# First self attention of a two-layer decoder: queries, keys and outputs by three fp32r products each, queries and keys by way of DRAM

## The reference

```python
xq = jnp.einsum('bsh,oh->bso', x, wq)
xk = jnp.einsum('bsh,oh->bso', x, wk)
xv = jnp.einsum('bsh,oh->bso', x, wv)
xq = xq.reshape(bsz, N_HEADS, seqlen, HEAD_DIM)
...
scores = jnp.einsum('bhid,bhjd->bhij', xq, xk) * SCALE
scores = jax.nn.softmax(scores, axis=-1)
out = jnp.einsum('bhij,bhjd->bhid', scores, xv)
out = out.reshape(bsz, seqlen, N_HEADS * HEAD_DIM)
return jnp.einsum('bso,ho->bsh', out, wo)
```

## Time and profile before

| | |
|---|---|
| median of 3 runs | 3024.14 us (3023.61 to 3031.14) |
| the profiled execution, whole | 3019.45 us |
| its span, first to last instruction | 3017.7 us |
| mean granted TensorE clock | 0.944 |
| TensorE busy | 2672.6 us, 89% |
| VectorE, ScalarE, GpSimd busy | 1675.6, 1177.9, 1563.1 us |
| DMA | 142460 packets, 238.12 MB |

### The profile page before, as it was taken

How to read it: one execution, slowest core, us unless ns; L and a number is a source line. 1 busy time by engine, 2 the same in 40 slices (tenths; PEclk the granted TensorE clock), 3 DMA queues, 4 the chain that set the end, 5 groups by cost and what they waited for, 6 DMA issues and landing times. The chain is left out here.

```text
span 3017.7 us, 40593 instructions
## 1 busy us (share of the span) xinstructions
PE 2672.6 (89%) x11441; PEld 1597.7 (53%) x11441; DVE 1675.6 (56%) x3323; ACT 1177.9 (39%) x1638; POOL 1563.1 (52%) x1298
## 2 busy tenths in 40 slices
PE   7999999999999999999999968982795588689696
PEld 5666666666666666666666533431574244333264
DVE  5665656655566556665665634662234555358753
ACT  3444444444444444444444324541222333345334
POOL 2666676667766677666766841224334212222353
PEclk9999999999999999999999979996897599899798
DMA  4333332333223332333323320003893100000143
GB/s 132 72 79 72 83 72 65 82 78 81 68 71 82 71 82 65 72 83 78 72 69 79 77 75 16 2 2 119 340 341 131 39 1 1 30 2 9 33 139 90
DMA packets 142460, 238.12 MB, mean 79 GB/s; under 512 B 27638, under 2 KB 72990, under 8 KB 137246
## 3 DMA queue, kind: packets, MB, share of 16 engines
q1 hardware_dynamic: 126510, 166.81, 22.2%
q0 software_dynamic: 11904, 64.06, 6.0%
q10 hardware_dynamic: 3952, 6.08, 0.6%
HBM read 89.52 MB, written 29.38 MB: 39 GB/s over the span
## 5 line engine op out<-in xcount | busy, mean ns | idle before, releaser
L636 POOL TENSOR_TENSOR a_total<-a_total,a_pr 128x1024 f32<-128x1024 f32 x384 | 912.6, 2377 | 70.3 <-ACT a_pr L620 49.9
L620 ACT ACTIVATE a_pr<-a_psS 128x1024 f32<-128x1024 f32 x512 | 525.1, 1026 | 650.2 <-PE a_psS L608 646.4
L567 DVE TENSOR_REDUCE a_nmax<-a_psX 128x1 f32<-128x512 f32 x1024 | 694.3, 687 | 149.7 <-PE a_psX L562 147.2
L648 PE MATMUL a_psO<-a_pr,a_vd 128*64 128x512 f32 x2048 | 481.8, 602 | 0.0
L562 PE MATMUL a_psX<-a_kA,a_qA 128*128 128x512 f32 x1024 | 412.3, 403 | 8.0 <-DMA a_kA<-a_klo 4.6
L636 POOL TENSOR_TENSOR a_total<-a_pr 128x1024 f32<-128x1024 f32 x64 | 152.9, 2388 | 507.1 <-ACT a_pr L620 507.1
L608 PE MATMUL a_psS<-a_qA,a_kA 128*128 128x512 f32 x1024 | 346.6, 420 | 1.6 <-DVE a_nT L583 1.4
L608 PE MATMUL a_psS<-a_qB,a_kB 128*128 128x512 f32 x1024 | 320.2, 394 | 0.7 <-DVE a_qB L591 0.7
L648 PEld LDWEIGHTS a_psO<-a_pr,a_vd 128*64 128x64 f32 x2048 | 129.9, 136 | 248.3 <-issue 212.0
L608 PEld LDWEIGHTS a_psS<-a_qA,a_kA 128*128 128x128 f32 x1024 | 183.7, 188 | 123.8 <-issue 90.1
L562 PEld LDWEIGHTS a_psX<-a_kA,a_qA 128*128 128x128 f32 x1024 | 191.9, 187 | 91.2 <-DVE a_nmax L567 16.5
(11 more groups left out here) (366 smaller groups left out, 4206.3 us busy)
## 6 DMA issues: line engine op xcount, KB each, us to landing
a_qA<-a_qhi SPq DMA_DIRECT2D x256, 128.0 KB, 2.3
a_kA<-a_khi SPq DMA_DIRECT2D x128, 128.0 KB, 2.3
a_kA<-a_klo SPq DMA_DIRECT2D x128, 128.0 KB, 2.3
a_kB<-a_khi SPq DMA_DIRECT2D x128, 128.0 KB, 2.3
a_qB<-a_qlo SPq DMA_DIRECT2D x128, 128.0 KB, 2.3
a_vd<-a_vg SPq DMA_DIRECT2D x128, 128.0 KB, 2.3
sorted_in<-g_zero SPq DMA_DIRECT2D x4, 1280.0 KB, 10.3
e_xg<-sorted_in SPq DMA_DIRECT2D x40, 128.0 KB, 7.5
```

The source lines that it names most:

```text
L567: w.eng.tensor_reduce(nmax[:, half, u:u + 1], psX[:, half, :], AX.X, ALU.max, negate=True)\
L620: w.eng.activation(pr[:, n, :], psS[:, half, :, :].rearrange("p a b -> p (a b)"), ACT.Exp, scale=SCALE)\
L636: w.eng.tensor_tensor(total[:, buf, :], first, pr[:, n, :], ALU.add).then_inc(sems["ad"], 1)
L648: last = w.eng.matmul(psO[q * HD:(q + 1) * HD, :], vd[:, b, kc, :], pr[:, n, q * 512:(q + 1) * 512], start=kc == 0, stop=kc == KC - 1)
```

## The change

Weights wq, wk and wo are split before the loop in a high part and a rest, as wv was. A piece of queries or keys is now six products (high with high, high with rest, rest with high, two halves of x), one of outputs 24. The parts of queries and keys go from a ring of four pieces (`ph`, `pl`) to DRAM, two transfers of 128 x 4 x 256 bytes per piece, and `build` reads six transfers of 256 KB from there; it waits for all stores issued before. The attention output is split by a new function, `split_out`, two units after it was computed. Output pieces move to place "1" of units 1 and 3, query and key pieces to other places, and the norm's parts move with them.

```diff
-        PLACES = [(3, "1"), (3, "3"), (3, "3b"), (3, "3c"), (3, "3d"), (0, "1"), (0, "3"), (0, "3b"),
-                  (1, "1"), (1, "3"), (1, "3b"), (1, "3c"), (1, "3d"), (2, "1"), (2, "2"), (2, "2b")]
+        PLACES = [(3, "3"), (3, "3b"), (3, "3c"), (3, "3d"), (0, "1"), (0, "2"), (0, "2b"), (0, "3"), (0, "3b"), (0, "3c"),
+                  (0, "3d"), (1, "3"), (1, "3b"), (1, "3c"), (1, "3d"), (2, "1")]
-            slots[0, "3d"] = slots[2, "3b"] = ("O",)
+            slots[1, "1"] = slots[3, "1"] = ("O",)
...
-                    for cc in range(2):
-                        last = w.eng.matmul(ps[:, 0:GT], wt[:, cc, c * P:(c + 1) * P], xT[:, cc, :],
-                                            start=cc == 0, stop=cc == 1)
+                    for n, (wp, xp) in enumerate(((hi, xh), (hi, xl), (lo, xh))):
+                        for cc in range(2):
+                            last = w.eng.matmul(ps[:, 0:GT], wp[:, cc, c * P:(c + 1) * P], xp[:, cc, :],
+                                                start=n == 0 and cc == 0, stop=n == 2 and cc == 1)
...
-                    for c in range(KC):
-                        last = w.eng.matmul(ps[:, 0:D], oT[:, buf, c, :], wo[:, c, :], start=c == 0, stop=c == KC - 1)
+                    for n, (op, wp) in enumerate(((oh, woh), (oh, wol), (ol, woh))):
+                        for c in range(KC):
+                            last = w.eng.matmul(ps[:, 0:D], op[:, buf, c, :], wp[:, c, :],
+                                                start=n == 0 and c == 0, stop=n == 2 and c == KC - 1)
...
                 if w.on("scalar"):
-                    if what == ("Q", 0) and not fresh:
-                        taken(w)
                     w.wait("mi", w.at("mi"))
-                    w.eng.activation(dst(hi), src, ACT.Copy).then_inc(sems["ch"], 1)
+                    w.wait(f"so{n}", w.at(f"so{n}"))
+                    w.eng.activation(ph[:, n, :], ps[:, 0:GT], ACT.Copy).then_inc(sems["ch"], 1)
...
+                if w.on("sync"):
+                    c, row = what[1], w.fixed(G * (GH * P))
+                    w.waits(("md", w.at("md", -1)))
+                    for t, src in ((qhi, ph), (qlo, pl)) if kind == "Q" else ((khi, ph), (klo, pl)):
+                        w.eng.dma_start(t[bass.ds(row, GH * P), c * HD:(c + 1) * HD].rearrange("(h p) t -> p h t", p=P),
+                                        src[:, n, :].bitcast(F32).rearrange("p (h t) -> p h t", t=HD)).then_inc(sems[f"so{n}"], 16)
...
-                w.waits(("md", w.at("md")), ("s", w.at("s")))
+                w.waits(("s", w.at("s")), *((f"so{n}", w.at(f"so{n}")) for n in range(PIECES)))
...
-                    for par in range(2):
-                        w.eng.dma_start(t[rows:rows + HD, b, par * 512:(par + 1) * 512].bitcast(F32),
-                                        src[par * HD:(par + 1) * HD, bass.ds(gbuf, 1), j, :].bitcast(F32)).then_inc(sems[f"{n}{b}"], 16)
+                    w.eng.dma_start(t[rows:rows + HD, b, :].bitcast(F32).rearrange("p (s n) -> p s n", n=512),
+                                    src[bass.ds(row, P), :].rearrange("(s p) n -> p s n", p=HD)).then_inc(sems[f"{n}{b}"], 16)
...
+        def split_out(w, j):
+
+            t, cols = j // 2, slice(j % 2 * HD, (j % 2 + 1) * HD)
+            if w.on("scalar"):
+                w.wait("ot", w.at("ot"))
+                w.wait("y", w.at("y"))
+                w.eng.activation(oh[:, t, :, cols], oT[:, :, :], ACT.Copy).then_inc(sems["oh"], 1)
+            w.inc("oh")
+            if w.on("vector"):
+                w.wait("oh", w.at("oh"))
+                w.eng.tensor_tensor(ol[:, t, :, cols], oT[:, :, :], oh[:, t, :, cols].bitcast(F32), ALU.subtract)\
+                    .then_inc(sems["ol"], 1)
+            w.inc("ol")
...
-                        if outs and kc == 2:
+                        if outs and kc == 6:
                             root(w, 1 if j == 1 else 0)
-                        if outs and kc == 5:
-                            norm_out(w, G - (j == 1), 1 if j == 1 else 0)
+                        if kc == 1 and (j == 2 or j == 0) and not first:
+                            norm_out(w, G - 1, 1 if j == 2 else 0)
...
-                        if outs and kc == 1:
+                        if outs and kc == 5:
                             moments(w, 1 if j == 1 else 0)
                         piece(f"k{kc}")
+                        if older and kc == 1:
+                            split_out(w, (j - 2) % GH)
```

More of the change, by code:

```diff
@@ L670, in turn_back, with divide @@
             w.inc("rec")
-        def divide(w, j):
+        def divide(w):
             if w.on("gpsimd"):
@@ L688, in group @@
                 old = not (first and j == 0)
+                older = not (first and j < 2)
                 def step(i):
@@ L704, in piece @@
                     ahead = 2 if task == ("T",) or j == 3 else 1
-                    if task is None or (not old if task[0] == "O" else ahead > left):
+                    if task is None or (first and j == 1 if task[0] == "O" else ahead > left):
                         return under
                     if task[0] == "O":
-                        misc(w, task, G - (j == 0), 1 if j == 0 else 0, bank=bank, back=under)
+                        misc(w, task, G - (j == 1), 1 if j == 1 else 0, bank=bank, back=under)
                     else:
```

102 lines of the change are left out of this document (50 added, 52 removed).

## The result

The changed kernel takes 3285.3 us (median, 3271.1 to 3288.7) against 3024.1 (3023.6 to 3031.1): a ratio of 1.084, interval 1.082 to 1.086. I had forecast 3104, 3045 to 3185. The direction was right and the mechanism in part, the size was not: 261 us came where I had 80. Neither of the two signs that I had named for a wrong forecast appeared: the search doesn't run at 0.70 through kc 2 and 3, and waits for DMA stand ahead of it in two of the four units from 500 to 620 us.

The account below looks back on a forecast made before the run. TensorE's work and waits were taken as the bound. Per group -4.0 + 1.5 + 0.95 + 6.1 = +4.6 us, 70 over the groups, with 10 before the loop +80: forecast 3104 us, range 3045 to 3185.

Parts of the forecast that it names:

- the two signs: Forecast wrong if the search runs at 0.70 through kc 2 and 3, or DMA waits precede it in every unit.
- What bounds the kernel: In the loop, what TensorE executes or waits for is the stage's time; it is busy 99.6 of 100 us.
- The products: fp32r products of 256 columns on TensorE take 0.120 us each, gaining 3.45 us per group.
- What moves away: VectorE's moments go behind reduction 11, gaining 0.25 us; unit 0's output piece no longer waits 0.3 us for its bank.
- What comes back at the unit's end: At the ends of units 0, 1 and 3 VectorE sets the next search's start: 1.5 us per group lost.
- The 0.95 us for unit 2's missing cover: Unit 2 loses its output piece, so the second score pass waits for the masked maxima: 0.95 us with x's subtraction.
- The split of the attention output: VectorE's `ol` after reduction 3 waits for ScalarE's copy and delays search matmul 6: 6.1 us per group, the largest term.
- The way over DRAM: Stores and loads of queries and keys fit beside the loop's work: cost 0 in the sum.
- the bound of 32 us: Upper bound for the DRAM way: 1 us in each of units 0 and 2, 32 us in all.
- Before the loop: Weight splits, 32 stores and the build put the first search at 45 us instead of 35.7: 10 us.
- The rival of the stores: Dear 256-byte stores or late builds cost 3 to 4 us per group and 25 at the beginning: 3185; chance 0.16.
- The split hides: Rival: `oh` is ready before reduction 3 ends, the split costs under 1 us per group: 3009 or 2995; chance 0.12.

Follow-up runs that it names:

- e1: The changed kernel with VectorE's subtraction `ol` on 128 x 64 columns in place of 128 x 512; 3238.6 us.
- e4: The changed kernel with GpSimd's add of kc 1 on 64 of 1024 columns; 3158.8 us.
- e11: The changed kernel with ScalarE's copy `oh` alone moved into the tail of the unit before; 3081.7 us.
- e2: The changed kernel with the copy `oh` moved into the tail of the unit before and subtraction `ol` moved from VectorE to GpSimd; 3065.5 us.
- e5: e2 with GpSimd's four operations for the root moved behind the last add, after the masked maxima are written; 3034.7 us.
- e8: e5 with the build at the end of unit 0 no longer waiting for the last four stored pieces of the next group; 3032.7 us.
- e9: e8 with the splits of the value and output weights moved behind all first projections; 3024.1 us, ratio 0.9988 to the kernel before.
- e14: e9 with the value pieces of units 0 and 1 at kc 7 and the splits of wq and wk in halves; 3028.2 us, ratio 0.9983.
- e12: e9 with four value pieces moved behind the last scores of units 0, 1 and 2, x's transposes last in the tail; 3031.1 us, ratio 1.0005.
- e10: e5 with query and key products in fp32 again, their DRAM way and places kept; 3045.7 us.
- e7: The kernel before the change with only the moments, root and normalised output moved; 3051.1 us.
- e6: The kernel before the change with only the way of queries and keys over DRAM added; 3031.9 us.

## Why the prediction missed

- **What bounds the kernel:** right. TensorE sets the end, and from the change over e1, e4, e11, e2, e5, e8 to e9 and e14 each version's stage is shorter as its waits ahead of the search are. e12 is the exception: its new waits stand elsewhere.
- **The products:** right, 0.12 us each. For the output 1.3 us per group (forecast 1.15). Of the 2.3 us for queries and keys 0.9 reached the loop's length (e10); with the 1.5 that come back at the units' ends, the sum had 0.8.
- **What moves away** is the first step that failed: "They go to behind reduction 11 [...]: 0.25 us gained." I followed the moments on VectorE and never the four operations of the root on GpSimd, from kc 2 to kc 6. There they delay the last add into the masked write. e5 puts it at 33.6 us of the stage; e7, with the moments and the normalised output moved too, at 20.0.
- **What comes back at the unit's end:** right for VectorE's part, as just said. The 0.95 us for unit 2's missing cover was a wait for the masked maxima; what stands there is a wait for loads, 1.2 us in e9's unit 2.
- **The split of the attention output** is the step that made the miss: "the subtraction, as `xl`, 0.68". `xl` runs while GpSimd is idle (it starts at 670.69 in unit 2's tail, and the last add ends at 667.07); `ol` was put just behind exponential 1, whose end starts GpSimd's add. The place and the chain over ScalarE held. The waits did not: 2.70, 2.87, 1.38 and 2.69 us in units 3, 0, 1 and 2 of one group, where I had 1.28, 1.87, 1.11 and 1.87, and unit 3 is off the most, because a copy that is earlier, but not early enough for the subtraction to start ahead of the add, only makes it stand longer. Without the add the term costs 94.5 us (e4 to e2; the sum had 95, partly by luck). With it, it costs 213 (the change to e2): 76 us more of idle TensorE, and 43 more of busy time at the lower clock, a term that the sum didn't have at all.
- **The way over DRAM:** hidden in the kernel before (e6), as said, with 9.5 us of waits; 36.7 in the change and 39.1 in e5, over the bound of 32 us that I had set.
- **Before the loop:** 17.5 us, not 10, and at a lower clock. The first store comes at 19.1 (16 + 2 in the sum), the stores take 25.0 us and not 20, and the build 7.4 and not 5. The single store was priced right; left out were the pauses of 3.1 and 2.0 us between them, behind the splits of wk and wv, and that a load lands after 4.1 to 5.2 us and not 2.3.

The sum by runs, on the stage's end: the split on VectorE 213.0 (forecast 95), the root 33.6 (0), all the rest 10.8 (forecast -15: -1.55 x 16 and 10): 257.4. The rival of the stores was given 0.16, and its own time of 3185 was the top of the range; the stores are not what happened. "The split hides" was nearer in one way: it named the copy's place as the switch, and e11 turned it.

The Trainium skill has the rule that I should have weighed. "SBUF — State Buffer", section "SBUF: two separate sides", says that VectorE and GpSimd share a pair of ports under an exclusive lock, that a VectorE operation with two SBUF inputs takes part in it, and that whoever comes second stands for the whole of the other's instruction. e4 and e11 agree: 692 and 682 ns where they don't meet, 1841 where they do. By that rule and the rows ahead of the forecast (exponential 1 from 675.44 to 676.47, an add behind it), the meeting could have been seen.

## What to carry to other kernels

Before a VectorE operation with two SBUF inputs is placed, look at what GpSimd runs at that time: price it at its length plus the rest of GpSimd's operation, and try first to have its input ready before GpSimd's turn. Follow every instruction of a moved step on its own engine, the four small ones on GpSimd too. And when an operation waits for another engine's copy, move the copy first: here 0.6 us of ScalarE's order was worth 200 us.
